# Graph attention on one core: TensorE turns and looks up the next step's edges ahead of this step's scatters

## The chip, the cores and the metric

The kernel runs on one core of a Trainium2 chip. The metric is the device time of one execution in microseconds. The core has five engines that run their own instruction streams in order and meet only at semaphores: TensorE (PE in the profile), VectorE (DVE), ScalarE (ACT), GpSimd (POOL) and SyncE (SP).

## The reference

Two blocks of a "metaformer" run over 8192 tokens of 128 numbers: row attention, a graph attention (GAT) that gates four experts, a mixing of rows, and eight routed experts. The change touches only the graph attention's pass over the edges:

```python
h = (x_flat @ W_gat).reshape(M, HEADS, NUM_EXPERTS)
a_src = (h * att_src).sum(-1)
a_dst = (h * att_dst).sum(-1)
e = jax.nn.leaky_relu(a_src[src] + a_dst[dst], negative_slope=0.2)
ee = jnp.exp(e - e_max[dst])
denom = jax.ops.segment_sum(ee, dst, num_segments=M)
alpha = ee / (denom[dst] + 1e-16)
msg = h[src] * alpha[:, :, None]
agg = jax.ops.segment_sum(msg, dst, num_segments=M)
```

There are 524288 edges. Their node numbers are drawn from 32768, while there are 8192 tokens. An index beyond the last token is held at the last token when it is read and dropped when it is written, so edges whose source is such a node all carry the last token's row.

## The kernel before

Earlier in the program the edges are compacted into keys. Edges whose source is a real token ("near") need their own source row; of the others only their number for each destination is wanted. The function `graph_edges` then runs through both lists.

**Near edges** go in steps of 16 columns of 128 edges. One step does this:

- POOL gathers the source rows with 16 indirect DMAs (L1000), one for each column, into `GS` (`sb_ge_gs`). It may start the gathers of step n once VectorE has decoded the keys of step n (semaphore `decoded`, raised at L1039, which VectorE does for step n in its step n-3) and has made the messages of step n-4.
- VectorE makes one-hot rows of the low and the high part of each destination: `OL` (`sb_ge_ol`, L1056, two buffers) and `OH` (`sb_ge_oh`, L1054).
- PE turns (transposes) `OL` into PSUM (`turn`, L1220, `p_turned`), ScalarE copies it to `OLT` (`sb_ge_olt`, L1013), and PE multiplies `OLT` with the table of destination terms (`look`, L1233, `p_look`). VectorE selects the wanted column (`select`, L1065 and L1068): this is a_dst[dst].
- `weigh` (L1077 to L1084) adds the gathered a_src and makes the exponent's argument; its first instruction waits for the gathers of its step. ScalarE does the exp (L1015), `message` (L1093) multiplies it with the gathered rows.
- VectorE spreads the messages over a window of destinations into `B` (`sb_ge_b`, L1103), and PE adds them up with `OL` as weights (`scatter`, L1242, `acc`).

**Counted edges** are added by products of bf16 one-hots, which VectorE makes (L1126) and PE multiplies (`count`, L1251).

A step has four chunks of four columns for `turn`, `look`, `scatter` and `B`. The steps are software-pipelined: while step n is scattered, step n+1 is turned and looked up. VectorE's order in step n is: for each chunk c, `B` of chunk c and, in most steps, the one-hots of a counted part; then `select` and `weigh` of step n+1, which wait for the last `look` of step n+1; then `OL` of step n+2, which waits for the last scatter of step n, as both use the same buffer; then `message` of step n+1. PE's order is written out in its own `step`, at the diff's lines. All order is that of the code; there is no scheduler.

In this run there are 24 steps: 16 with counting, 4 without, then 4 with counting again. Three short trips of counting alone come first.

Of the kernel before, what the change touches and what calls it, by code (L numbers as in the profile page):

```python
# [912 lines left out]
def graph_edges(nc, sem, KEYS_D, KC, SRC_T, DT, TRIPS, SUMS, CN, LAST, last_in, ident):  # L913
# [4 lines left out]
    CHUNKS = STEP // CHUNK  # L918
# [3 lines left out]
    with ExitStack() as ctx:  # L922
# [42 lines left out]
        def counts(engine):  # L965

            return trips(engine, 0, UNITS // 4, 1), trips(engine, 1, TMAX, 1), trips(engine, 2, UNITS, 3)
# [3 lines left out]
        @block.sync  # L971
        def _(sp):
            sp.dma_start(LAST[:, :], SRC_T[TOKENS - 1, :].partition_broadcast(P)).then_inc(last_in, 16)
            n_both, n_gather, n_rest = counts(sp)

            def load(t, u, first):
                if not first:
                    sp.wait_ge(decoded, t * STEPS + 2 * u - 2)
                at = t * 2 + u if first else nc.s_assert_within(t * 2 + u, 0, 2 * MOST - 1, skip_runtime_bounds_check_because=
                                                                "the trips are made from the number of near keys")  # L980
                sp.dma_start(KB[:, u, :], KEYS_D[ds(at * P, P), :]).then_inc(keys_in[u], 16)

            for u in range(2):
                load(0, u, True)
            with sp.Fori(1, n_both + n_gather + 1) as t:
                for u in range(2):
                    load(t, u, False)
# [218 lines left out]
        @block.tensor  # L1206
        def _(pe):
            n_both, n_gather, n_rest = counts(pe)
            zero = KC[:, KCOLS - P:]
            zeros = zero.unsqueeze(1).to_broadcast([P, BANK // P, P])  # L1210

            def turn(t, j, c):

                t, j = t + j // STEPS, j % STEPS
                n = t * STEPS + j
                if c == 0:
                    pe.wait_ge(ol_made, n + 1)
                pe.wait_ge(turned_out, n * CHUNKS + c + 1)
                for k in range(CHUNK):
                    last = nc.tensor.transpose(TURNED[:, c % 2, k * P:(k + 1) * P], OL[:, j % 2, c * CHUNK + k, :], ident[:, :])  # L1220
                last.then_inc(turned, 1)

            def look(t, j, c):

                t, j = t + j // STEPS, j % STEPS
                n = t * STEPS + j
                if c == 0:
                    pe.wait_ge(selected, n + 1)
                pe.wait_ge(turned_out, n * CHUNKS + c + 1 + AHEAD_T)
                q = (j % 2) * 2 + c // 2  # L1230
                for k in range(CHUNK):
                    at = ((c % 2) * CHUNK + k) * GHEADS * WIN
                    last = nc.tensor.matmul(LOOK[:, c // 2, at:at + GHEADS * WIN], OLT[:, c, k * P:(k + 1) * P],  # L1233
                                            DT[:, :, q * WIN:(q + 1) * WIN], start=True, stop=True)
                last.then_inc(looked, 1)

            def scatter(n, j, c):

                pe.wait_ge(b_made, n * CHUNKS + c + 1 + AHEAD)
                q = (j % 2) * 2 + c // 2  # L1240
                for k in range(CHUNK):
                    last = nc.tensor.matmul(ACC[:, q, 0:WIN * PART], OL[:, j % 2, c * CHUNK + k, :],  # L1242
                                            B[:, c, k, :, :].rearrange("p x w -> p (x w)"), start=False, stop=False, skip_group_check=True)
                last.then_inc(b_free, 1)

            def count(g, q):

                pe.wait_ge(hot_made, g + 1)
                for a in range(PAIRS):
                    for i in range(2):  # L1250
                        last = nc.tensor.matmul(COUNT, CL[:, q, a, :, i], CH[:, q, a, :, i], start=False, stop=False,  # L1251
                                                skip_group_check=True)
                last.then_inc(hot_free, 1)

            def step(t, j, counted, more):
                n = t * STEPS + j
                for c in range(CHUNKS):
                    scatter(n, j, c)
                    if more:
                        turn(t, j + 1, c)  # L1260
                        if c > 0:
                            look(t, j + 1, c - 1)
                    if counted is not None:
                        if c == CHUNKS - 1 and more:
                            look(t, j + 1, c)
                        count(counted + (j * CPS + c), c % NC)
                    elif c == CHUNKS - 1 and more:
                        look(t, j + 1, c)

            pe.sem_inc(b_free, NB)  # L1270
            pe.sem_inc(hot_free, NC)
            pe.sem_inc(turned_out, AHEAD_T)
            pe.sem_inc(looked, AHEAD_L)
            for q in range(QUARTERS):
                nc.tensor.matmul(ACC[:, q, :], zero, zeros, start=True, stop=False, skip_group_check=True)
            for c in range(CHUNKS):
                turn(0, 0, c)
                if c > 0:
                    look(0, 0, c - 1)
            look(0, 0, CHUNKS - 1)  # L1280
            with pe.Fori(0, n_rest) as i:
                for c in range(CPS):
                    count(i * CPS + c, c % NC)
            with pe.Fori(0, n_both) as t:
                for j in range(STEPS):
                    step(t, j, n_rest * CPS + t * (STEPS * CPS), True)
            with pe.Fori(0, n_gather) as i:
                for j in range(STEPS):
                    step(n_both + i, j, None, True)
            for j in range(STEPS):  # L1290
                step(n_both + n_gather, j, n_rest * CPS + n_both * (STEPS * CPS), j < STEPS - 1)
            for q in range(QUARTERS):
                last = nc.tensor.matmul(ACC[:, q, :], zero, zeros, start=False, stop=True, skip_group_check=True)
            last.then_inc(acc_done, 1)
# [731 lines left out]
```

## Time and profile before

| what | value |
|---|---|
| median of 3 runs | 2399.8 us (2399.08 to 2400.2) |
| the profiled execution's own time | 2394.67 us |
| its span in the trace | 2392.9 us |
| PE busy in the span | 1734.6 us (72%) |
| DVE busy | 1633.5 us (68%) |
| ACT busy | 748.9 us (31%) |
| POOL busy | 736.9 us (31%) |
| granted PE clock, mean of the span | 0.889 of full speed |

The span is what the trace holds of one execution, and the program's other parts (attention, experts, mixing) lie in it before and behind the edge pass. Times in the rows below are microseconds from the span's start. The edge pass goes from the first gather at 909.83 to the copy of its sums at 1560.23.

### The profile page before, as it was taken

To read this page: it belongs to the slowest core of one execution; us is meant where nothing else is said; L and a number is where in the kernel's file an instruction comes from. 1 tells how busy PE (TensorE), PEld (TensorE's weight loads), DVE (VectorE), ACT (ScalarE), POOL (GpSimd) and SP (SyncE) were. 2 spreads that over 40 slices of the span, in tenths; PEclk is the share of its full clock that TensorE was granted. 3 is DMA by queue.
4 is the path that set the end of the run, shared out by engine and by line. 5 is a ranking of instruction groups with operands and counts; after the bars stand their busy time and mean duration, and the time that the engine had idled before them with its cause. 6 is when DMAs were issued, how large, how long until landed. Compare 5 with 4: busy or idle time off the path is not lost. (4 is left out here: it accounts for less than half of the span.)

```text
span 2392.9 us, 34125 instructions
## 1 busy us (share of the span) xinstructions
PE 1734.6 (72%) x10531; PEld 1329.2 (56%) x10531; DVE 1633.5 (68%) x3612; ACT 748.9 (31%) x2069; POOL 736.9 (31%) x541
## 2 busy tenths in 40 slices
PE   0042069999999856767776776729999499849997
PEld 0042047877887655555554554606667466726665
DVE  7999967777777647677767746754445323567777
ACT  3120047766766520100110010014343212324342
POOL 0581022332332106778878777000000000300000
PEclk9999999999999856887888788869999689669999
DMA  7000000000000020000000111000000811000000
GB/s 281 0 2 3 0 12 0 0 0 0 0 0 0 1 12 7 8 8 7 7 7 7 7 8 7 1 18 1 18 18 18 185 31 31 0 18 18 18 18 18
DMA packets 73271, 47.39 MB, mean 20 GB/s; under 512 B 25553, under 2 KB 69378, under 8 KB 72706
## 3 DMA queue, kind: packets, MB, share of 16 engines
q1 hardware_dynamic: 58914, 41.73, 6.8%
q0 software_dynamic: 12288, 3.96, 2.6%
q10 hardware_dynamic: 2016, 1.06, 0.2%
q8 instruction: 27, 0.44, 0.1%
q14 instruction: 26, 0.21, 0.0%
HBM read 33.21 MB, written 13.50 MB: 20 GB/s over the span
## 5 line engine op out<-in xcount | busy, mean ns | idle before, releaser
L1000 POOL DMA_INDIRECT sb_ge_gs<-source_rows,sb_ge_idx x384 | 466.8, 1216 | 126.9 <-issue 116.1
L1242 PE MATMUL acc<-sb_ge_b,sb_ge_ol 128*128 128x320 f32 x768 | 275.7, 510 | 188.5 <-DVE sb_ge_b L1103 188.5
L1566 DVE SCALAR_TENSOR_TENSOR sb_X<-x_py,sb_x_gc,sb_X 128x128 f32 (+1 forms) x768 | 269.4, 351 | 187.2 <-PE x_py L1506 160.8
L1495 PE MATMUL x_pu<-sb_TT,sb_x_w 128*128 (+1 forms) x512 | 248.1, 609 | 78.2 <-PEq L1521 76.2
L1242 PEld LDWEIGHTS acc<-sb_ge_b,sb_ge_ol 128*128 128x128 f32 x768 | 162.6, 223 | 253.2 <-DVE sb_ge_b L1103 191.5
L1506 PEld LDWEIGHTS x_py<-sb_x_w,sb_x_ht 128*128 128x128 f32 x2048 | 248.1, 192 | 60.8 <-issue 39.5
L235 POOL TENSOR_TENSOR sb_bias<-sb_PB,sb_TT 128x1024 f32<-128x1024 f32 x64 | 151.2, 2363 | 337.6 <-DVE sb_logits L262 337.6
L1485 ACT ACTIVATE sb_x_ht<-x_pu,sb_x_b 128x512 f32<-128x512 f32 x256 | 174.4, 687 | 252.4 <-PE x_pu L1495 252.2
L1506 PE MATMUL x_py<-sb_x_w,sb_x_ht 128*128 128x128 f32 x2048 | 249.6, 275 | 1.3 <-DVE sb_X L1566 1.3
L1013 ACT ACTIVATE sb_ge_olt<-p_turned 128x512 f32<-128x512 f32 x96 | 57.4, 598 | 458.7 <-PE p_turned L1220 450.5
L319 ACT ACTIVATE sb_probs<-sb_logits,sb_neg_max 128x128 f32<-128x128 f32 x512 | 198.4, 390 | 7.0 <-DVE sb_neg_max L273 3.7
L1495 PEld LDWEIGHTS x_pu<-sb_TT,sb_x_w 128*128 128x128 f32 x512 | 88.4, 193 | 170.8 <-issue 85.3
L780 POOL TENSOR_TENSOR sb_X<-sb_t_xn,sb_X 128x512 f32 x16 | 20.4, 1272 | 508.1 <-DVE sb_t_xn L797 508.1
L1065 DVE TENSOR_TENSOR sb_ge_sel<-p_look,sb_ge_oh 128x1024 f32<-128x1024 f32 x24 | 29.4, 1225 | 171.9 <-PE p_look L1233 171.9
L1103 DVE TENSOR_TENSOR sb_ge_b<-sb_ge_oh,sb_ge_msg 128x1280 f32<-128x1280 f32 x96 | 142.1, 1484 | 1.6 <-DVE sb_ge_c_digits L1119 0.7
L262 DVE SCALAR_TENSOR_TENSOR sb_logits<-p_logits,sb_bias 128x1024 f32<-128x1024 f32 x64 | 78.4, 1225 | 71.1 <-PE p_logits L365 71.1
L365 PE MATMUL p_logits<-sb_kT,sb_qT 128*128 128x512 f32 x256 | 123.5, 605 | 3.4 <-issue 3.4
L401 PE MATMUL p_out<-sb_v,sb_probsT 128*128 128x32 f32 x1024 | 119.9, 271 | 0.5 <-ACT sb_probsT L327 0.5
L401 PEld LDWEIGHTS p_out<-sb_v,sb_probsT 128*128 128x128 f32 x1024 | 119.5, 192 | 1.0 <-ACT sb_probsT L327 1.0
L279 DVE COPY sb_kT<-p_xn 32x256 f32<-32x256 f32 x256 | 107.5, 420 | 17.1 <-PE p_xn L390 12.4
L1126 DVE TENSOR_TENSOR sb_ge_c_onehot_lo<-sb_ge_iota,sb_ge_c_digits 128x2048 bf16<-128x2048 bf16 x92 | 111.9, 1216 | 0.1
L415 PE MATMUL p_xn<-sb_ident,sb_xn 128*128 128x128 f32 x64 | 17.8, 279 | 129.7 <-DVE sb_xn L256 126.7
(337 smaller groups left out, 3205.9 us busy)
## 6 DMA issues: line engine op xcount, KB each, us to landing
sb_ge_gs<-source_rows,sb_ge_idx POOLq DMA_INDIRECT x384
sb_z<-in_L_conv_z SPq DMA_DIRECT2D x1, 4096.0 KB, 20.4
sb_TT<-in_L_conv_mask SPq DMA_DIRECT2D x1, 4096.0 KB, 42.8
x_rows<-sb_X SPq DMA_DIRECT2D x4, 1024.0 KB, 5.1
normed_rows<-sb_TT SPq DMA_DIRECT2D x4, 1024.0 KB, 6.5
sb_X<-x_rows SPq DMA_DIRECT2D x2, 2048.0 KB, 20.7
sb_mr_xg<-normed_rows SPq DMA_DIRECT2D x16, 256.0 KB, 3.4
out<-sb_X SPq DMA_DIRECT2D x8, 512.0 KB, 5.3
```

Of the source, the lines that this page charges most:

```text
L235: nc.gpsimd.tensor_tensor(BM[:, u, :, :], PB[:, :, :], MB[:, ds(s * T, T)].unsqueeze(1).to_broadcast([P, HEADS, T]), ALU.add).then_inc(bia ...
L319: last = nc.scalar.activation(PR[:, u, h, :], LG[:, h, :], ACT.Exp, bias=NM[:, h:h + 1], accum_out=SM[:, u, h:h + 1])
L365: last = nc.tensor.matmul(L[:, j, :], QT[:, j, :], KT[:, j, :, :].rearrange("p r k -> p (r k)"), start=True, stop=True)
L401: last = nc.tensor.matmul(O[:, h * DH:(h + 1) * DH], PT[:, h, :], V[:, 1 - u, h * DH:(h + 1) * DH], start=True, stop=True)
L1000: pool.indirect_dma_start(GS[:, j, k, :], None, SRC_T, bass.IndirectOffsetOnAxis(ap=IDX[:, j, k:k + 1], axis=0))\
L1103: nc.vector.tensor_tensor(B[:, c, :, :, :], OH[:, j % 2, k, :].unsqueeze(3).to_broadcast(shape), MSG[:, j % 2, k, :].unsqueeze(2).to_broad ...
L1126: last = nc.vector.tensor_tensor(out[:, q, :, :, :], iota_2[:, 0:wide, :].unsqueeze(1).to_broadcast(shape), digit.rearrange("p (a i) -> p ...
L1242: last = nc.tensor.matmul(ACC[:, q, 0:WIN * PART], OL[:, j % 2, c * CHUNK + k, :], B[:, c, k, :, :].rearrange("p x w -> p (x w)"), start=F ...
L1485: nc.scalar.activation(HT[:, u, c, :], PU[c % 2][:, :], ACT.Gelu, bias=bb1[:, c:c + 1])\
L1495: nc.tensor.matmul(PU[c % 2][:, :], w1[:, c * P:(c + 1) * P], TT[:, ds(g * BANK, BANK)], start=True, stop=True)\
L1506: last = nc.tensor.matmul(bank[:, (e % 4) * C:(e % 4 + 1) * C], HT[:, u, e * chunks + c, k * P:(k + 1) * P], w2[:, e * chunks + c, :], sta ...
L1566: last = nc.vector.scalar_tensor_tensor(out=xs, in0=PY[(k * YB + b) % NY][:, (e % 4) * C:(e % 4 + 1) * C], scalar=GC[:, u, k * experts + e ...
```

## The change

Only PE's order inside a step changes; no instruction is added or removed.

```diff
             def step(t, j, counted, more):
                 n = t * STEPS + j
+                if more:
+                    turn(t, j + 1, 0)
+                    turn(t, j + 1, 1)
                 for c in range(CHUNKS):
                     scatter(n, j, c)
-                    if more:
-                        turn(t, j + 1, c)
-                        if c > 0:
-                            look(t, j + 1, c - 1)
+                    if more and c < CHUNKS - 1:
+                        look(t, j + 1, c)
+                        if c + 2 < CHUNKS:
+                            turn(t, j + 1, c + 2)
+                        else:
+                            look(t, j + 1, c + 1)
                     if counted is not None:
-                        if c == CHUNKS - 1 and more:
-                            look(t, j + 1, c)
                         count(counted + (j * CPS + c), c % NC)
-                    elif c == CHUNKS - 1 and more:
-                        look(t, j + 1, c)
```

The head of a counted step on PE, before. In the rows `acc<-sb_ge_b` is a scatter, `p_turned` a turn, `p_look` a look and `acc<-sb_ge_c_onehot_hi` a count; `ISA` and `REGISTER_ALU` are waits and counters.

```order
L1242 MATMUL acc<-sb_ge_b,sb_ge_ol 128x320 x4
L1217 REGISTER_ALU
L1218 ISA
L1220 MATMUL p_turned<-sb_ident,sb_ge_ol 128x128 x4
L1248 REGISTER_ALU
L1251 MATMUL acc<-sb_ge_c_onehot_hi,sb_ge_c_onehot_lo 128x64 x16
```

The first scatter came first, then the first turn. The same place on PE with the change:

```order
L1217 REGISTER_ALU
L1218 ISA
L1220 MATMUL p_turned<-sb_ident,sb_ge_ol 128x128 x4
L1218 REGISTER_ALU
L1220 MATMUL p_turned<-sb_ident,sb_ge_ol 128x128 x4
L1242 MATMUL acc<-sb_ge_b,sb_ge_ol 128x320 x4
L1229 REGISTER_ALU
L1233 MATMUL p_look<-sb_DT,sb_ge_olt 128x64 x4
L1220 MATMUL p_turned<-sb_ident,sb_ge_ol 128x128 x4
L1248 REGISTER_ALU
L1251 MATMUL acc<-sb_ge_c_onehot_hi,sb_ge_c_onehot_lo 128x64 x16
```

Two turns now stand ahead of the first scatter, and a look follows it. The end of a counted step on PE, before:

```order
L1242 MATMUL acc<-sb_ge_b,sb_ge_ol 128x320 x4
L1220 MATMUL p_turned<-sb_ident,sb_ge_ol 128x128 x4
L1229 REGISTER_ALU
L1233 MATMUL p_look<-sb_DT,sb_ge_olt 128x64 x4
L1229 REGISTER_ALU
L1233 MATMUL p_look<-sb_DT,sb_ge_olt 128x64 x4
L1248 REGISTER_ALU
L1251 MATMUL acc<-sb_ge_c_onehot_hi,sb_ge_c_onehot_lo 128x64 x16
```

The fourth scatter stood ahead of the last turn and the last two looks. The same place with the change:

```order
L1242 MATMUL acc<-sb_ge_b,sb_ge_ol 128x320 x4
L1229 REGISTER_ALU
L1233 MATMUL p_look<-sb_DT,sb_ge_olt 128x64 x4
L1229 REGISTER_ALU
L1233 MATMUL p_look<-sb_DT,sb_ge_olt 128x64 x4
L1248 REGISTER_ALU
L1251 MATMUL acc<-sb_ge_c_onehot_hi,sb_ge_c_onehot_lo 128x64 x16
L1242 MATMUL acc<-sb_ge_b,sb_ge_ol 128x320 x4
L1248 REGISTER_ALU
L1251 MATMUL acc<-sb_ge_c_onehot_hi,sb_ge_c_onehot_lo 128x64 x16
```

The last look now stands right behind the third scatter, ahead of the third count, the fourth scatter and the fourth count.

## Rows read from the trace of the kernel before

**Rows 1.** The page's costliest groups: busy and mean ns, idle before and its releaser.
```profile
L1000 POOL DMA_INDIRECT sb_ge_gs<-source_rows,sb_ge_idx x384 | 466.8, 1216 | 126.9 <-issue 116.1
...
L1065 DVE TENSOR_TENSOR sb_ge_sel<-p_look,sb_ge_oh 128x1024 f32<-128x1024 f32 x24 | 29.4, 1225 | 171.9 <-PE p_look L1233 171.9
```

**Rows 2.** DVE over time, a counted step and one without: start, length, idle before.
```profile
993.74 0.22 DVE L1077 TENSOR_TENSOR sb_ge_a<-sb_ge_d,sb_ge_gs 128x64 f32<-128x64 f32 x1
...
995.25 2.28 DVE L1056 TENSOR_TENSOR sb_ge_ol<-sb_ge_iota_i,sb_ge_lo 128x2048 f32<-128x2048 int32 x1
...
997.90 1.49 DVE L1103 TENSOR_TENSOR sb_ge_b<-sb_ge_oh,sb_ge_msg 128x1280 f32<-128x1280 f32 x1
...
1010.17 0.68 DVE L1126 TENSOR_TENSOR sb_ge_c_onehot_hi<-sb_ge_iota,sb_ge_c_digits 128x1024 bf16<-128x1024 bf16 x1
1018.26 1.22 DVE L1065 TENSOR_TENSOR sb_ge_sel<-p_look,sb_ge_oh 128x1024 f32<-128x1024 f32 x1 [7.41 <-PE p_look L1233]
...
1020.77 0.22 DVE L1077 TENSOR_TENSOR sb_ge_a<-sb_ge_d,sb_ge_gs 128x64 f32<-128x64 f32 x1
...
1410.70 1.23 DVE L1065 TENSOR_TENSOR sb_ge_sel<-p_look,sb_ge_oh 128x1024 f32<-128x1024 f32 x1 [11.42 <-PE p_look L1233]
...
1434.67 1.22 DVE L1065 TENSOR_TENSOR sb_ge_sel<-p_look,sb_ge_oh 128x1024 f32<-128x1024 f32 x1 [11.35 <-PE p_look L1233]
```

**Rows 3.** PE over time in the same counted step.
```profile
999.44 4.64 PE L1242 MATMUL acc<-sb_ge_b,sb_ge_ol 128*128 128x320 f32 x8 [7.77 <-DVE sb_ge_b L1103]
1003.87 1.06 PE L1220 MATMUL p_turned<-sb_ident,sb_ge_ol 128*128 128x128 f32 x4
1004.73 1.04 PE L1251 MATMUL acc<-sb_ge_c_onehot_hi,sb_ge_c_onehot_lo 128*128 128x64 bf16 x16
1005.60 2.40 PE L1242 MATMUL acc<-sb_ge_b,sb_ge_ol 128*128 128x320 f32 x8
1007.83 0.60 PE L1220 MATMUL p_turned<-sb_ident,sb_ge_ol 128*128 128x128 f32 x4
...
1009.60 2.40 PE L1242 MATMUL acc<-sb_ge_b,sb_ge_ol 128*128 128x320 f32 x8
...
1016.26 1.96 PE L1233 MATMUL p_look<-sb_DT,sb_ge_olt 128*128 128x64 f32 x16
```

**Rows 4.** The gathers' tile: the first user of each step's rows, and POOL's waits.
```profile
L1077 DVE TENSOR_TENSOR sb_ge_a<-sb_ge_d,sb_ge_gs x24: 224/225/237, 942.1 to 1539.8; 128x64 f32<-128x64 f32 x24
...
  DVE sb_ge_hi L1039: 10.8, 3
```

**Rows 5.** POOL over time: single gathers, with the first and the last of 384.
```profile
909.83 1.30 POOL L1000 DMA_INDIRECT sb_ge_gs<-source_rows,sb_ge_idx  x1 [4.08 <-DVE sb_ge_hi L1039]
...
1025.62 1.55 POOL L1000 DMA_INDIRECT sb_ge_gs<-source_rows,sb_ge_idx  x1 [0.30 <-issue]
...
1038.94 0.94 POOL L1000 DMA_INDIRECT sb_ge_gs<-source_rows,sb_ge_idx  x1 [0.31 <-issue]
...
1341.02 1.90 POOL L1000 DMA_INDIRECT sb_ge_gs<-source_rows,sb_ge_idx  x1 [0.30 <-issue]
...
1365.27 3.05 POOL L1000 DMA_INDIRECT sb_ge_gs<-source_rows,sb_ge_idx  x1 [0.30 <-issue]
...
1472.73 3.15 POOL L1000 DMA_INDIRECT sb_ge_gs<-source_rows,sb_ge_idx  x1 [5.11 <-DVE sb_ge_hi L1039]
...
1498.33 1.09 POOL L1000 DMA_INDIRECT sb_ge_gs<-source_rows,sb_ge_idx  x1 [0.30 <-issue]
```

**Rows 6.** Busy time in short stretches behind the last gather.
```profile
core 0: us, PE busy (x) PEld busy (x) DVE busy (x) ACT busy (x) POOL busy (x), PEclk, DMA share, GB/s
...
1501.00:1501.40 0.40, 0.40 (x6) 0.40 (x5) 0.40 (x1) 0.36 (x1) 0.00 (x0) 1.00 0.06 5
1501.40:1501.80 0.40, 0.40 (x16) 0.40 (x15) 0.40 (x2) 0.00 (x0) 0.00 (x0) 1.00 0.00 0
```

**Rows 7.** DVE at the end of the edge pass.
```profile
1560.23 1.68 DVE L1200 COPY sb_SUMS<-acc 128x320 f32<-128x320 f32 x4 [6.03 <-PE acc L1293]
```

## The prediction

> **What bounds the kernel now.** I read the page's costliest groups first. VectorE's wait ahead of `select` (L1065) is the largest it has in the edge pass: 171.9 us over 24 steps, all put down to PE's `look` at L1233 [rows 1]. The same list shows POOL's 384 gathers with 466.8 us of work and 126.9 us idle, nearly all of it "issue", so POOL hardly waits for anyone [rows 1].
>
> Then VectorE over time. In a counted step it starts `weigh` (L1077) at 993.74 and again at 1020.77, 27.0 us later. Its last one-hot ends at 1010.85, and `select` starts at 1018.26 after 7.41 us of idling [rows 2]. A step without counting takes 24.0 us and idles 11.4 us [rows 2]. PE over time shows why: it waits 7.77 us for the first `B`, and then works without a gap from 999.44 until the last looks of 1016.26 [rows 3]. So VectorE and PE take turns: VectorE waits for the last look, PE for the first `B`. This chain sets the pace. On average a step takes (1539.8 - 942.1) / 23 = 26.0 us [rows 4].
>
> The third view is POOL over time, and it decides what the change is worth. The first gather starts at 909.83 and the last ends at 1498.33 + 1.09 = 1499.42 [rows 5]: 589.6 us for 24 steps, 24.6 us per step. Its waits for VectorE are 10.8 us in 3 pieces, of which 4.08 us stand ahead of the first gather [rows 4, 5]. Hence 6.7 us lie inside, 5.11 us of them at 1472.73, ahead of the last step's gathers [rows 5]. POOL is nearly as slow as the chain that paces the kernel: it has 1.4 us per step to spare.
>
> **The change on the chain.** It adds and removes no instruction. From the first `B` (999.44) to `select` (1018.26) PE takes 18.82 us now [rows 3, 2]. With the new order three things lie there:
> - Chunk 0: a scatter at the lower clock, 1003.87 - 999.44 = 4.43 us, then a look, a turn and a count. In a warm chunk these three take 4.00 - 2.23 = 1.77 us (1009.60 - 1005.60, less 1007.83 - 1005.60) [rows 3]. Sum 6.20 us.
> - Chunk 1: scatter, look, turn, count, 4.00 us.
> - Chunk 2: scatter 2.23 us and two looks with the hop to VectorE, 1018.26 - 1016.26 = 2.00 us. Sum 4.23 us.
>
> That makes 14.4 us, 4.4 us less. Gone from this stretch are the fourth scatter, the third count, and the two turns that now stand ahead. If the lower clock lasts through all of chunk 0 the three short pieces take twice as long (now the turn takes 0.86 us there against 0.44 warm), and the gain is 2.6 us. The two turns wait for `OL` of the next step, which VectorE ends some 1.9 us before the first `B` is ready: 995.25 + 2.28 = 997.5 against 999.4 [rows 2, 3]. Two turns at the lower clock are 1.7 us. They fit, narrowly; were they late, it would be by tenths. The chain would fall from 27.0 to between 22.6 and 24.4 us in a counted step. In one without counting a scatter and two turns leave the stretch, 3.1 us, and 24.0 becomes 20.9 us.
>
> ScalarE's copies follow the turns earlier and are in time: `look` 0 and 1 have a scatter ahead of them, and the turns of chunks 2 and 3 a scatter more. The fourth scatter now ends later relative to `select`, and `OL` of two steps on waits for it, but it ends about 2.7 us after the last look, while `select`, its reduction and `weigh` take 1020.77 - 1018.26 + 1.2 = 3.7 us before `OL` starts [rows 2]. So this wait stays covered. SP's key loads wait for decodes only.
>
> **The gathers take over.** A gather that no VectorE work disturbs takes 0.94 + 0.31 = 1.25 us (at 1038.94), 16 of them 19.9 us. While VectorE makes `B` and counted one-hots they are longer: the eight from 1025.62 to 1038.94 take 13.3 us against 10.0, so 3.3 us more per counted step. Beside `OL` one takes 1.90 or 3.05 us, depending on where it starts: 1.0 to 2.1 us more per step [rows 5]. A counted step thus costs POOL 19.9 + 3.3 + 1.0 to 2.1 = 24.2 to 25.3 us. That is more than the chain's 22.6 to 24.4. The chain can gain 2.6 to 4.4 us a step, but `weigh` must have the gathered rows, and POOL becomes the bound from the first or second step on.
>
> The Trainium skill, SBUF — State Buffer, Who interferes with whom, says that a VectorE instruction with two SBUF inputs contends with a GpSimd instruction that reads SBUF. By that rule, the trace agrees: the stretched gathers lie beside L1056, L1103 and L1126. The same section infers that `tensor_tensor` leaves descriptor generation alone, which would give 19.9 us per step; the rows above show 24.6 and decide against it.
>
> The sum goes by POOL's own total. Now: 589.6 us. The waits inside go: -6.7. POOL then works alongside VectorE work that it now misses, since it runs up to three steps ahead at the end: half the chunks of step 21, all of step 22, two chunks of step 20 and the rest of an `OL`, about 1.7 + 3.3 + 1.6 + 0.6 = 7 us at the prices above. Where `OL` falls among the gathers becomes fixed: `weigh` starts when the rows are there, `OL` 1.5 us later (995.25 - 993.74) [rows 2]. The DMA engines fall idle 2.0 us after the last gather ends (1501.4 against 1499.42) [rows 6, 5], which I take as the landing time. `OL` then starts 3.5 us after a step's gathers end, half way through the third gather of the next step. The extra rises from 1.0 us, if `OL` starts as a gather does, to 2.1 just before the next: here 1.6 us, against about 1.5 us on average now; 22 times 0.1 is +2. Total 589.6 - 6.7 + 7 + 2 = 592, so the last gather ends at 1502 and the last `weigh` starts at 1504 instead of 1539.8 [rows 4]. From there to the copy of the sums (1560.23 [rows 7]) nothing changes, 20.4 us. **The saving is 1539.8 - 1504 = 36 us.**
>
> The profiled execution would fall from 2394.7 to 2358.7 us. The median of the runs shown is 5.1 us above that execution, so I forecast 2399.8 - 36 = **2363.8 us**.
>
> **Rivals.**
> - *POOL gives way and the chain stays the bound.* For it speaks that the gathers' length depends on VectorE's work beside them. Against it: that work is the same per step. The saving would be 23 steps of 2.6 to 4.4 us, 60 to 101 us, at most 2340 us and about 2320. Chance 5%.
> - *Denser VectorE work stretches the gathers more.* At 2.1 us for each `OL` the sum loses 22 x 0.5 = 11 us; a landing of up to 5.9 us (the first step's gathers ended 5.9 us ahead of its `weigh`, the only upper bound I have) takes 4 more. Saving 15 to 25 us, 2375 to 2385. Chance 12%.
> - *PE stays at the lower clock, and the kernel is slower.* The granted level falls in PE's 7.8 us gap: the scatter takes 4.43 us at 1.2 GHz against 2.23 at 2.4 GHz [rows 3]. Two turns as the first work behind the gap might not bring it back, or more pauses for `B` might keep it low. If the whole stretch ran so, 14.4 would be 7.97 + 8.0 + 8.3 = 24.3 us, a step 32.5 us, and the kernel some 120 us slower. It becomes a loss once PE's stretch is 3.4 us longer than 14.4 us. Against it: PE's idle share per step stays near the present one, and it now recovers within two pieces of work. Chance 4%. The Trainium skill, TensorE: Matmul & The Clock Gate, Part 4, has transposes not counting as work for the gate; then the clock would rise as now, counted from the scatter, which is my 24.4 us bound.
> - *The turns at the head arrive late and hold the scatters, and nothing is won.* It would need `OL` 3 to 4 us later. VectorE makes it before `message` and `B`, so I see no way. About 2399. Chance 3%.
>
> **How the numbers follow.** The forecast has 76%. Its own range is the `OL` price from 1.0 to 2.1 us (-13, +11) and the landing: savings of 22 to 49 us, 2351 to 2378. The range on record reaches a little into the second rival: 2350 to 2380. A difference of 0.2% (4.8 us) is what a measurement of this kernel can tell from no change. Faster by more than that: 76 + 5 + 12 = 93%; within it 2% (most of the fourth rival), slower 5%.
>
> **What the profile should show.** The wait of L1065 for PE should shrink from 171.9 us to under 80. VectorE should idle ahead of L1077 instead, for the gathers' DMA. POOL should have no wait for L1039 but the first, and its last gather should end near 1502, at most 2 to 3 us ahead of the last `weigh`. PE's turns should start right behind `OL`, before the first `B`. I am wrong if VectorE still waits for PE longer than for the gathers, if POOL's total falls below 575 or rises above 605 us, or if the lower clock covers more than the first chunk of each step.

## The result and the profile after

| | before | with the change |
|---|---|---|
| median | 2399.62 us (4 runs, 2399.08 to 2400.2) | 2356.01 us (4 runs, 2354.29 to 2357.76) |
| the profiled execution's own time | 2394.67 us | 2355.66 us |
| its span | 2392.9 us | 2353.9 us |
| first gather to the copy of the sums | 650.4 us | 608.9 us |

The ratio is 0.9818 (95% interval 0.9801 to 0.9835), 43.6 us less by the medians. The two profiled executions differ by 39.0 us, as that of before was 5 us faster than its median. A second measurement of the changed kernel, below, has the ratio 0.9836. The edge pass itself became 41.5 us shorter; in the profiled execution of the changed kernel it starts 3.4 us later.

The page's groups and the views of the two tiles `sb_ge_gs` and `sb_ge_sel` after the change come first; they answer to [rows 1] and [rows 4]. The columns are as there.

```profile
L1000 POOL DMA_INDIRECT sb_ge_gs<-source_rows,sb_ge_idx x384 | 470.0, 1224 | 120.8 <-issue 116.7
...
L1220 PE MATMUL p_turned<-sb_ident,sb_ge_ol 128*128 128x128 f32 x384 | 76.0, 350 | 131.1 <-DVE sb_ge_ol L1056 131.1
```

```profile
L1000 POOL DMA_INDIRECT sb_ge_gs<-source_rows,sb_ge_idx x384: 940/1098/3062, 913.2 to 1499.0; - x192
L1077 DVE TENSOR_TENSOR sb_ge_a<-sb_ge_d,sb_ge_gs x24: 224/225/226, 945.4 to 1502.5; 128x64 f32<-128x64 f32 x24
...
  DMA sb_ge_gs<-source_rows,sb_ge_idx: 54.4, 22
  DVE sb_ge_hi L1039: 4.1, 1
```

```profile
its engine sat idle before it (us, times) until:
  PE p_look L1233: 77.4, 23
```

The last fence is the tile `sb_ge_sel`: VectorE's wait for the look fell from 171.9 to 77.4 us. A wait that did not exist before took its place, 54.4 us at the first user of the gathered rows, in 22 of 24 steps. POOL waits for VectorE only once, ahead of its first gather.

VectorE over time in one counted step, which answers to [rows 2]:

```profile
1006.96 0.68 DVE L1126 TENSOR_TENSOR sb_ge_c_onehot_hi<-sb_ge_iota,sb_ge_c_digits 128x1024 bf16<-128x1024 bf16 x1
1008.96 1.23 DVE L1065 TENSOR_TENSOR sb_ge_sel<-p_look,sb_ge_oh 128x1024 f32<-128x1024 f32 x1 [1.33 <-PE p_look L1233]
1010.22 1.22 DVE L1068 TENSOR_REDUCE sb_ge_d<-sb_ge_sel 128x64 f32<-128x1024 f32 x1
1015.04 0.22 DVE L1077 TENSOR_TENSOR sb_ge_a<-sb_ge_d,sb_ge_gs 128x64 f32<-128x64 f32 x1 [3.60 <-DMA sb_ge_gs<-source_rows,sb_ge_idx]
```

After 1.33 us for the look VectorE does its 2.5 us of select and reduction and then stands still for 3.60 us until the rows are there. PE over time in the same step, against [rows 3]:

```profile
994.45 1.96 PE L1220 MATMUL p_turned<-sb_ident,sb_ge_ol 128*128 128x128 f32 x8 [6.53 <-DVE sb_ge_ol L1056]
996.23 2.96 PE L1242 MATMUL acc<-sb_ge_b,sb_ge_ol 128*128 128x320 f32 x8
999.03 1.00 PE L1233 MATMUL p_look<-sb_DT,sb_ge_olt 128*128 128x64 f32 x8
...
1007.03 1.89 PE L1233 MATMUL p_look<-sb_DT,sb_ge_olt 128*128 128x64 f32 x16
...
1018.91 1.96 PE L1220 MATMUL p_turned<-sb_ident,sb_ge_ol 128*128 128x128 f32 x8 [6.78 <-DVE sb_ge_ol L1056]
1020.69 4.37 PE L1242 MATMUL acc<-sb_ge_b,sb_ge_ol 128*128 128x320 f32 x8
```

The two turns start right behind `OL` and take 1.78 us, and the first scatter follows without a gap. It takes 2.80 us in this step (996.23 to 999.03) and 4.21 us in the next, where a look starts at 1024.90: the lower clock ends at another point of it. POOL and the end of the pass, against [rows 5] and [rows 7]:

```profile
1016.25 1.15 POOL L1000 DMA_INDIRECT sb_ge_gs<-source_rows,sb_ge_idx  x1 [0.31 <-issue]
1017.70 1.90 POOL L1000 DMA_INDIRECT sb_ge_gs<-source_rows,sb_ge_idx  x1 [0.30 <-issue]
...
1499.01 0.95 POOL L1000 DMA_INDIRECT sb_ge_gs<-source_rows,sb_ge_idx  x1 [0.30 <-issue]
```

```profile
1502.49 0.22 DVE L1077 TENSOR_TENSOR sb_ge_a<-sb_ge_d,sb_ge_gs 128x64 f32<-128x64 f32 x1 [3.59 <-DMA sb_ge_gs<-source_rows,sb_ge_idx]
...
1522.12 1.68 DVE L1200 COPY sb_SUMS<-acc 128x320 f32<-128x320 f32 x4 [5.28 <-PE acc L1294]
```

The last `weigh` follows the end of the last gather (1499.96) by 2.5 us. Before, it followed by 40 us (1539.8 against 1499.42).

### The profile page after: what moved, and what is told of

The parts are those of the page before. It is cut to its first block and busy times, and to the rows that moved or that the text cites. A ratio compares the mean times of both kernels' runs of the same rounds, so it can differ in the third digit from the quotient of the medians.

```text
span 2353.9 us, 34125 instructions
## 1 busy us (share of the span) xinstructions
PE 1742.2 (74%) x10531; PEld 1338.7 (57%) x10531; DVE 1633.4 (69%) x3612; ACT 748.4 (32%) x2069; POOL 739.9 (31%) x541
## 5 line engine op out<-in xcount | busy, mean ns | idle before, releaser
L1000 POOL DMA_INDIRECT sb_ge_gs<-source_rows,sb_ge_idx x384 | 470.0, 1224 | 120.8 <-issue 116.7
L1242 PE MATMUL acc<-sb_ge_b,sb_ge_ol 128*128 128x320 f32 x768 | 266.1, 496 | 15.2 <-DVE sb_ge_b L1103 15.1
L1242 PEld LDWEIGHTS acc<-sb_ge_b,sb_ge_ol 128*128 128x128 f32 x768 | 158.9, 218 | 81.0 <-issue 23.1
L1220 PE MATMUL p_turned<-sb_ident,sb_ge_ol 128*128 128x128 f32 x384 | 76.0, 350 | 131.1 <-DVE sb_ge_ol L1056 131.1
L1103 DVE TENSOR_TENSOR sb_ge_b<-sb_ge_oh,sb_ge_msg 128x1280 f32<-128x1280 f32 x96 | 142.1, 1484 | 1.6 <-DVE sb_ge_c_digits L1119 0.7
L1220 PEld LDWEIGHTS p_turned<-sb_ident,sb_ge_ol 128*128 128x128 f32 x384 | 60.4, 189 | 136.1 <-issue 129.6
L279 DVE COPY sb_kT<-p_xn 32x256 f32<-32x256 f32 x256 | 107.6, 420 | 17.2 <-PE p_xn L390 12.5
```

Of the source, the lines that this page charges most:

```text
L1000: pool.indirect_dma_start(GS[:, j, k, :], None, SRC_T, bass.IndirectOffsetOnAxis(ap=IDX[:, j, k:k + 1], axis=0))\
L1103: nc.vector.tensor_tensor(B[:, c, :, :, :], OH[:, j % 2, k, :].unsqueeze(3).to_broadcast(shape), MSG[:, j % 2, k, :].unsqueeze(2).to_broad ...
```

## The experiments

Each ratio is to the kernel before on the same chip, with its 95% interval. In the code, `...` stands for lines left out.

### Which part of the new order brings the saving

First, the changed kernel with the last look behind the last scatter:

```diff
-                    if more and c < CHUNKS - 1:
+                    if more:
                         look(t, j + 1, c)
                         if c + 2 < CHUNKS:
                             turn(t, j + 1, c + 2)
-                        else:
-                            look(t, j + 1, c + 1)
```

> The changed kernel with one part undone: the two turns stay at the head of a step, but the last look stands behind the last scatter again. VectorE's select then comes one scatter and one count later, 2.23 + 0.49 = 2.7 us a step. Theory (the gathers set the pace since the change, and the chain of VectorE and PE had 54.4 / 22 = 2.5 us a step to spare ahead of L1077): the added 2.7 us fill the spare time, 2356 to 2370 us, and the wait of L1077 for the gathers falls from 54 us to under 15. Rival (the chain still sets the pace): 23 steps of 2.7 us, 2415 to 2420 us, slower than the kernel before.

Measured: 2363.08 us, ratio 0.9857 (0.9841 to 0.9874). The two tiles, `sb_ge_gs` and then `sb_ge_sel`:

```profile
  DMA sb_ge_gs<-source_rows,sb_ge_idx: 4.6, 7
```

```profile
  PE p_look L1233: 133.0, 23
```

The look is waited for 133.0 us instead of 77.4, so 55.6 us went into this wait, and 49.8 of them came out of the wait for the rows (54.4 to 4.6). The kernel lost only 7 us (2363.08 against 2356.01 and 2355.91 in the two measurements of the changed kernel). A chain that set the pace would have lost some 60.

Second, the turns behind the first scatter, all looks still ahead of the last scatter; the diff is against the changed kernel:

```diff
-                if more:
-                    turn(t, j + 1, 0)
-                    turn(t, j + 1, 1)
                 for c in range(CHUNKS):
                     scatter(n, j, c)
-                    if more and c < CHUNKS - 1:
-                        look(t, j + 1, c)
-                        if c + 2 < CHUNKS:
-                            turn(t, j + 1, c + 2)
-                        else:
-                            look(t, j + 1, c + 1)
+                    if more and c == 0:
+                        turn(t, j + 1, 0)
+                        turn(t, j + 1, 1)
+                    if more and c == 1:
+                        look(t, j + 1, 0)
+                        turn(t, j + 1, 2)
+                    if more and c == 2:
+                        look(t, j + 1, 1)
+                        turn(t, j + 1, 3)
+                        look(t, j + 1, 2)
+                        look(t, j + 1, 3)
```

> The other part undone: the turns come behind the first scatter again (two there, then one each), while all looks still stand ahead of the last scatter. From the first B to select PE has 2.5 us more a step than in the changed kernel (two turns and a wait for ScalarE's copy of the last one). Theory (gathers set the pace, 2.5 us to spare): 2356 to 2370 us, so either part alone brings nearly the whole saving. Rival (the turns at the head make the saving): at least 2400 us.

Measured: 2356.94 us, ratio 0.9836 (0.982 to 0.9853), the same as the full change in its second measurement. L1077 waits 17.2 us for the rows. Either half of the change is thus enough for nearly all of the saving, and the turns at the head add nothing that can be measured once the looks stand ahead of the last scatter.

### What sets the pace

Every second gather was left out, in the changed kernel and in the kernel before. The rows that are not gathered stay zeros, which VectorE writes once, so these two kernels do less than the reference asks; VectorE waits for half the count. The edit to the changed kernel, which is the same in the other:

```diff
-                    for k in range(STEP):
+                    for k in range(0, STEP, 2):
...
+            nc.vector.memset(GS[:, :, :, :], 0.0)
...
-                    v.wait_ge(gathered[j][h], (t + 1) * 16 * SLOT)
+                    v.wait_ge(gathered[j][h], (t + 1) * 16 * (SLOT // 2))
```

> The changed kernel with the gathers of every second column left out (its output is thus not the reference's; the missing rows are zeros that VectorE writes once, about 1 us). POOL's work falls from 24.4 to about 12 us a step. Theory (gathers set the pace): the wait of L1077 (54.4 us) vanishes and the chain paces the kernel at about 21.9 us a step, 2300 to 2310 us. Rival (the chain sets the pace already): 2350 to 2358 us.

Measured: 2303.23 us, ratio 0.9605 (0.9589 to 0.9621). `weigh` has no wait left, and `select` waits 82.2 us.

> The kernel before with the gathers of every second column left out in the same way. Theory (there the chain of VectorE and PE set the pace at 26.0 us a step, and POOL had 1.4 us a step to spare): no gain, 2398 to 2402 us. Rival (gathers also cost the kernel before something, by slowing other work beside them or in single steps): 2370 to 2390 us.

Measured: 2396.89 us, ratio 0.9999 (0.9989 to 1.0008). L1065, here L1066, waits 173.2 us, against 171.9 in [rows 1]. The same cut of POOL's work is worth 53 us with the new order and nothing with the old one. The bound has moved from the chain of VectorE and PE to the gathers. The page's row of the gathers with half of them, in the changed kernel and then in the kernel before:

```profile
L1000 POOL DMA_INDIRECT sb_ge_gs<-source_rows,sb_ge_idx x192 | 286.5, 1492 | 216.7 <-DVE sb_ge_hi L1040 164.9
```

```profile
L1000 POOL DMA_INDIRECT sb_ge_gs<-source_rows,sb_ge_idx x192 | 263.9, 1375 | 317.3 <-DVE sb_ge_hi L1040 265.5
```

At 0.943 us each, 192 gathers would take 181 us. They take 105 us more with the new order and 83 us more with the old one. All 384 take 108 and 105 us more than 384 times 0.943. So the extra follows neither the number of gathers nor VectorE's work, which is nearly the same in all four; it depends on which of VectorE's instructions the gathers fall beside. In both half runs POOL now waits for the decodes, and in 17 steps of each the first two gathers behind that wait take about 3.15 and 2.90 us, as the one at 1472.73 does in [rows 5]. These 34 gathers hold 70.7 us of the extra in each run. Of the rest, gathers beside `OL` make 22 us with the new order (15 of them) and 2 us with the old one (2 of them).

### Why the gathers take 24.4 us a step

`OL` made twice by VectorE in the changed kernel:

```diff
+        twice = sem("ge_twice")
...
+                nc.vector.tensor_tensor(OL[:, j % 2, :, :], iota_i[:, :].unsqueeze(1).to_broadcast([P, STEP, P]),
+                                        LO[:, j, :].unsqueeze(2).to_broadcast([P, STEP, P]), ALU.is_equal).then_inc(twice, 1)
+                v.wait_ge(twice, n + 1)
                 nc.vector.tensor_tensor(OL[:, j % 2, :, :], iota_i[:, :].unsqueeze(1).to_broadcast([P, STEP, P]),
```

> The changed kernel in which VectorE makes the one-hots OL (L1056, two inputs in SBUF) twice, 2.3 us more VectorE work a step. VectorE has 2.5 us a step to spare ahead of L1077. Theory (VectorE's work with two SBUF inputs holds up the gathers beside it, and these set the pace): each gather beside the doubled OL is longer by the 2.2 us more, 24 x 2.2 = 53 us, 2400 to 2412 us, and the gathers' mean goes from 1224 to about 1360 ns. Rival (the gathers have their length whatever VectorE does, so only spare time is used up): 2356 to 2366 us.

Measured: 2383.66 us, ratio 0.9951 (0.9934 to 0.9968), 28 us slower than the changed kernel beside it. That lies between the two: half of the theory's 53 us, and more than the rival allows. VectorE and POOL over time around the two `OL` instructions:

```profile
1021.16 2.28 DVE L1057 TENSOR_TENSOR sb_ge_ol<-sb_ge_iota_i,sb_ge_lo 128x2048 f32<-128x2048 int32 x1
1022.03 2.23 POOL L1001 DMA_INDIRECT sb_ge_gs<-source_rows,sb_ge_idx  x1 [0.30 <-issue]
1023.47 2.29 DVE L1060 TENSOR_TENSOR sb_ge_ol<-sb_ge_iota_i,sb_ge_lo 128x2048 f32<-128x2048 int32 x1
1024.56 2.02 POOL L1001 DMA_INDIRECT sb_ge_gs<-source_rows,sb_ge_idx  x1 [0.30 <-issue]
```

Each `OL` here holds up the one gather that starts while it runs, until 0.82 us after its end (1023.44 to 1024.26, 1025.76 to 1026.58). The gather that had started at 1020.78, ahead of the first `OL`, took its 0.94 us. Between the two instructions a held gather gets through. So a second `OL` costs one more held gather, 2.02 - 0.94 = 1.1 us in this step, and not its own 2.2 us; 24 times 1.1 to 1.2 is the 27 us by which the gathers' total grew (470.0 to 496.8 us).

The reduction behind select done three times:

```diff
+        twice = sem("ge_twice")
...
+                for r in range(2):
+                    nc.vector.tensor_reduce(DV[:, :, :], SEL[:, :, :, :], AX.X, ALU.add).then_inc(twice, 1)
+                    v.wait_ge(twice, n * 2 + r + 1)
                 nc.vector.tensor_reduce(DV[:, :, :], SEL[:, :, :, :], AX.X, ALU.add).then_inc(sums, 1)
```

> The changed kernel in which VectorE does the reduction behind select (L1068, one input in SBUF) three times, 2.5 us more VectorE work a step, ahead of the wait for the gathers. Theory (work with one SBUF input leaves the gathers alone, and the spare time takes it): 2356 to 2368 us, with the gathers' mean still at 1224 ns and the wait of L1077 under 15 us. Rival (any VectorE work holds the gathers up, or the chain sets the pace): 2395 to 2415 us.

Measured: 2363.78 us, ratio 0.9863 (0.9846 to 0.9879). The gathers' mean is 1230 ns, against 1224, and the wait of L1081, this kernel's `weigh`, 1.7 us, against 54.4. A little more VectorE time than with `OL` twice (2.44 us a step against 2.28) costs 8 us instead of 28: the spare time took it, and the gathers hardly changed.

The numbers 0 to 127 in a free corner of PSUM, in the changed kernel:

```diff
+        IOTA_P = ACC[:, 1, WIN * PART:WIN * PART + P]
+        LOF = local("lof", [P, STEPS, STEP])
+        zeroed = sem("ge_zeroed")
...
+                nc.vector.tensor_copy(LOF[:, j, :], LO[:, j, :])
...
-                nc.vector.tensor_tensor(OL[:, j % 2, :, :], iota_i[:, :].unsqueeze(1).to_broadcast([P, STEP, P]),
-                                        LO[:, j, :].unsqueeze(2).to_broadcast([P, STEP, P]), ALU.is_equal).then_inc(ol_made, 1)
+                nc.vector.tensor_tensor(OL[:, j % 2, :, :], IOTA_P.unsqueeze(1).to_broadcast([P, STEP, P]),
+                                        LOF[:, j, :].unsqueeze(2).to_broadcast([P, STEP, P]), ALU.is_equal).then_inc(ol_made, 1)
...
+            v.wait_ge(zeroed, 1)
+            nc.vector.tensor_copy(IOTA_P, iota_f[:, :]).then_inc(iota_cast, 1)
+            v.wait_ge(iota_cast, 3)
...
```

> The changed kernel with the row of numbers 0 to 127 that OL is compared with held in a free corner of PSUM, so that L1056 has one SBUF input in place of two; a copy of 0.2 us a step turns the low digits to f32. Theory (two SBUF inputs hold up the gathers): the 1.4 us by which gathers are longer beside OL go, the gathers take 23.0 us a step, the chain becomes the bound in some steps, 2325 to 2338 us. Rival (the length beside OL has another cause, such as OL's writes): 2354 to 2360 us.

Measured: 2325.52 us, ratio 0.9697 (0.968 to 0.9714). VectorE and POOL over time around `OL`:

```profile
1036.64 2.28 DVE L1060 TENSOR_TENSOR sb_ge_ol<-acc,sb_ge_lof 128x2048 f32<-128x2048 f32 x1
1037.51 0.94 POOL L1003 DMA_INDIRECT sb_ge_gs<-source_rows,sb_ge_idx  x1 [0.30 <-issue]
1038.76 0.94 POOL L1003 DMA_INDIRECT sb_ge_gs<-source_rows,sb_ge_idx  x1 [0.30 <-issue]
```

`OL` is as long as before, 2.28 us, but the gather that starts inside it takes 0.94 us. The gathers' total fell by 30.8 us to 439.2, and the kernel by 30.4. The edit also turned `OL`'s inputs from int32 to f32, but the type is not what held the gathers: in the changed kernel all 92 gathers that start inside `B` (L1103, f32, both inputs in SBUF) take more than 1 us, and all 48 that start inside `select` (L1065, f32, one input in PSUM) or the reduction (L1068, one input) take 0.94 to 0.95. The Trainium skill, SBUF — State Buffer, Who interferes with whom, says that an instruction of VectorE with two SBUF inputs contends with a GpSimd instruction that reads SBUF; these rows agree. The same section infers that this leaves descriptor generation alone. For these gathers, which take their indices from SBUF, the measurement decides against that.

> The changed kernel once more, for the same chip as the runs beside it: ratio to the kernel before 0.981 to 0.984.

Measured, on the same chip as the last three runs: 2355.91 us, ratio 0.9836 (0.9819 to 0.9852).

The same two edits on the kernel before:

> The kernel before (PE's old order) with the numbers 0 to 127 in PSUM, so that the gathers are shortened as in the run on the changed kernel, where it gave 30 us. Theory (before the change the chain of VectorE and PE sets the pace, and POOL's work is hidden): 2394 to 2400 us, no change; only the new order makes shorter gathers worth anything. Rival (shorter gathers help by themselves): 2365 to 2375 us.

Measured: 2571.95 us, against 2550.88 us for the kernel before on that chip, ratio 1.0057 (1.0026 to 1.0088). This chip ran both kernels some 150 to 175 us slower than the others did, so the run says little, and it was repeated beside the changed kernel with the same edit.

> The kernel before with the numbers 0 to 127 in PSUM once more, as the chip of the first run showed a lower granted clock and some 150 us more for the kernel before as well. Theory: ratio to the kernel before 0.998 to 1.003. Rival (shorter gathers help by themselves): ratio 0.985 to 0.991.

Measured: 2397.08 us, ratio 1.0004 (0.9994 to 1.0014). POOL and VectorE in the two tiles, `sb_ge_gs` and `sb_ge_sel`:

```profile
  DVE sb_ge_hi L1042: 34.8, 9
```

```profile
  PE p_look L1240: 168.8, 23
```

> The changed kernel with the numbers in PSUM once more, beside it: ratio to the kernel before 0.968 to 0.972.

Measured: 2324.7 us, ratio 0.9696 (0.968 to 0.9713). With the old order the shorter gathers only made POOL wait 34.8 us for VectorE's decodes. With the new order they are worth 30 us. This is the fastest of the versions that make all gathers.

## Why the prediction was right, point by point

- **The chain.** In the two steps shown the way from `weigh` to the end of the next reduction takes 1011.44 - 990.58 = 20.9 us and 22.3 us, against 22.6 to 24.4 us as predicted. Over 19 counted steps it takes 20.5 to 24.3 us, 22.0 on average, so the term was a little too long. The first scatter, up to the start of the next piece, takes 3.8 us on average where I had put 4.43; before the change it took 4.1. The turns ahead of it make the difference: the scatters' busy time (L1242) is 275.7 us before and 277.7 in the run with the turns behind the first scatter, and 266.1, 268.8 and 264.2 us in the changed kernel, in its second measurement and in the run with the last look late, where the turns stand ahead. So the bound of 24.4 us, by which the clock would rise as before, counted from the scatter, is reached in single steps and is not the rule. A step without counting takes 20.4 to 20.9 us up to that point, against 20.9.
- **The gathers take over.** Shown by the runs with half the gathers, and by the 54.4 us wait at L1077, which I had named. They take over in the third step's rows: the first two `weigh` do not wait.
- **One sign of being wrong came true.** I had written that I am wrong if VectorE still waits for PE longer than for the gathers, and it does: 77.4 us at L1065 against 54.4 us at L1077. The sign was badly chosen. The gathers set when `weigh` ends, and with it when `OL` and `B` let PE start, so the wait for the look stays in each step whatever sets the pace. What tells is the wait that ends last, ahead of `weigh`, and the runs that shorten one side alone. The other two signs stayed away: POOL's total lies between 575 and 605 us, and the turns behind the first scatter take 0.44 to 0.45 us, as at the higher clock, in all but one of the records.
- **The saving, 36 us, was too small by some 5 us in the edge pass.** The term that was mis-sized is POOL's total, 592 us predicted and 586.7 measured. The waits that go, 6.7 us, were right. The 7 us for VectorE work that POOL would newly meet and the 2 us for where `OL` falls together measured 3.2 us (470.0 - 466.8 us in the gathers). The gathers that end 0.82 us behind an `OL` are 31.6 us longer than 0.943 us each before and 31.4 us now, so the second term is nothing and the first is about 3. I had counted two chunks of step 20 as missed by POOL before. It did idle beside them, up to 1472.73, but the two gathers behind that wait took 3.15 and 2.90 us, 4.2 us of extra for the two chunks left where my price was 1.7, so part of the 7 us was already paid. And the rows of a step are there 1.6 us after its last gather, in most steps, not 2.0. `OL` thus starts earlier in the gather beside it, and most steps pay 1.0 to 1.4 us for it, not 1.6. Against that, the landing grows to 2.5 us in the last steps. What follows the last `weigh` is 19.6 us, 0.8 less than predicted.
- **The median** moved by 43.6 us, 7.6 more than forecast. 5.5 of them are the edge pass, less 2.5 us outside it, and 4.6 are an offset: the profiled execution lay 4.95 us below its median before and 0.35 us below it now, while the sum took the offset to be the same on both sides.
- **The rival with the clock** did not come. The mean granted clock rose from 0.889 to 0.897. PE's gap behind the last count moved from the wait for `B` to the wait for `OL`; the same step shows 6.53 us there against 7.77.
- **The rival of denser VectorE work** did not come either: the mean gather went from 1216 to 1224 ns.
- **Turns too late.** In the two steps shown the turns end at 996.23 and 1020.69, and the first `B` is ready at 996.17 and 1020.64 (its instruction starts at 994.68 and 1019.15 and takes 1.49 us). The cover is used up and overrun by 0.05 us, within the tenths that I had allowed.

## What to carry to other kernels

When two engines wait for each other in turns, look at what a third engine needs per step before pricing a cut in their loop: here 94.5 us came out of the wait for the look (171.9 to 77.4) and 54.4 us came back as a wait for gathers. A bound that has taken over can then be attacked itself, and an edit that was worth nothing before (0.0%) is worth 1.3% now. Of an order change with two parts, try each part alone: here either was nearly enough.

## What the runs showed of the hardware

- A gather by indirect DMA takes POOL 0.94 us plus 0.30 us of issue. One that starts while VectorE runs `OL` or `B`, both with two SBUF inputs, ends only 0.82 us after that instruction or, at times, after a later one of the kind; beside one with an input in PSUM it takes 0.94 us. A second `OL` right behind the first costs one more held gather, 1.1 us, and not its own 2.2 us.
- The sum of these delays depends on what the gathers fall beside: 105 and 108 us for 384 gathers, 83 and 105 us for 192. Behind a wait for the decodes in a counted step two gathers in a row take 3.15 and 2.90 us, up to 0.82 us behind the second one-hot after the `B` beside which they start. Why they are held through three instructions, and a gather beside `B` otherwise mostly through one, was not tried.
- In the changed kernel the gathered rows are there 1.5 to 1.9 us after the gather's end in the steps up to 1310 us in which VectorE waits for them, and 2.2 to 2.6 us after it in the later ones. The share of busy DMA engines is 0.08 to 0.09 up to 1280 us and 0.15 from 1340 us on. Why the packets take longer there was not tried.
